# Counting edges tile by tile: each tile of 128 edges multiplied once, into PSUM banks of 50 destinations

## The reference

```python
HW = h @ W
row, col = (edge_index[0], edge_index[1])      # src, dst
s = HW @ a[:OUT_F, 0]
t = HW @ a[OUT_F:, 0]
e = leaky_relu(s[row] + t[col], 0.2)
m = segment_max(e, row)
ex = exp(e - m[row])
den = segment_sum(ex, row)
att = ex / den[row]
agg = segment_sum(att[:, None] * h[col], row)
basis = _b_splines(agg, grid)                  # 8 cubic splines on each feature
out = silu(agg) @ base_w.T + einsum('nip,oip->no', basis, spline_w)
x = layernorm(x + out)
```

## Time and profile before

| | us |
|---|---|
| median of 3 runs | 429.96 (428.74 to 430.42) |
| the profiled execution | 430.31 |
| its span, first to last instruction | 428.5 |

### The profile page before, as it was taken

One profiled execution on the slowest core, in us unless ns is written; L12 is line 12 of the kernel. 1 busy time (PEld: TensorE's weight loads), 2 busy tenths in 40 slices (PEclk: granted clock), 3 DMA queues, 4 the chain that ended last, 5 costly groups with the idle time before them and its releaser, 6 DMA issues.

```text
span 428.5 us, 5227 instructions
## 1 busy us (share of the span) xinstructions
PE 399.4 (93%) x1881; PEld 306.0 (71%) x1881; DVE 367.2 (86%) x457; ACT 274.0 (64%) x299; POOL 33.1 (8%) x162
## 2 busy tenths in 40 slices
PE   3999995299999999999999999999999999999994
PEld 0436563288888888878778888888777777777772
DVE  7968999997868867799988999989799969999645
ACT  7535675456456659788659586678646785779212
POOL 5100000100000000001100110101011010101000
PEclk9999999589999999999999999999999999999998
DMA  8980000600000000955454636363242346371303
GB/s 265 376 201 2 2 0 0 198 0 2 0 0 2 1 2 6 337 173 144 151 165 134 192 102 194 113 182 89 67 139 50 98 124 194 101 217 50 98 1 115
DMA packets 23452, 45.91 MB, mean 107 GB/s; under 512 B 1831, under 2 KB 2043, under 8 KB 23427
## 3 DMA queue, kind: packets, MB, share of 16 engines
q0 software_dynamic: 11088, 21.44, 18.6%
q1 hardware_dynamic: 12338, 24.14, 17.9%
HBM read 43.02 MB, written 2.56 MB: 106 GB/s over the span
## 4 chain that ended last, share of the span: by engine, by line
PE 54%; issue 29%; DVE 9%; POOL 3%; DMA 3%; ACT 0%; DVEq 0%; POOLq 0%
PE PS L1113 24%; PE PS L1069 17%; PE PS L1013 5%; POOL wh L374 3%; PE PS L1052 3%; DVE still L414 2%; DMA wh<-in_splT 2%; PE PS L989 2%; DVE oh L394 1%; DVE xl L502 1%; PE PS L968 1%; PE PS L1079 1%; DVE wl L593 1%; DMA ei<-in_edges 1%; DVE ex L629 0%
## 5 line engine op out<-in xcount | busy, mean ns | idle before, releaser
L1113 PE MATMUL PS<-wh,s 128*128 128x512 f32 (+1 forms) x720 | 225.2, 392 | 2.3 <-ACT s L884 1.1
L1113 PEld LDWEIGHTS PS<-wh,s 128*128 128x128 f32 (+1 forms) x720 | 133.4, 185 | 36.4 <-ACT s L884 3.5
L1113 PE MATMUL PS<-wl,s 128*128 128x512 f32 (+1 forms) x360 | 141.1, 392 | 0.0
L884 ACT ACTIVATE s<-v 128x1280 fp32r<-128x1280 f32 (+1 forms) x32 | 40.0, 1250 | 63.9 <-DVE v L701 58.9
L1113 PEld LDWEIGHTS PS<-wl,s 128*128 128x128 f32 (+1 forms) x360 | 66.8, 185 | 15.2
L1013 PE MATMUL PS<-oh,still 128*128 128x320 bf16 x304 | 45.4, 304 | 9.9 <-DVE still L414 7.9
L695 DVE SCALAR_TENSOR_TENSOR v<-v,v 128x1280 f32<-128x1280 f32 (+1 forms) x32 | 46.5, 1454 | 4.8 <-ACT v L870 4.8
L1013 PEld LDWEIGHTS PS<-oh,still 128*128 128x128 bf16 x304 | 28.8, 99 | 29.6 <-DVE still L414 9.6
L701 DVE SCALAR_TENSOR_TENSOR v<-v,v 128x1280 f32<-128x1280 f32 (+1 forms) x32 | 46.8, 1461 | 3.3
L711 DVE SCALAR_TENSOR_TENSOR s<-v,s 128x1280 fp32r<-128x1280 f32 (+1 forms) x32 | 46.5, 1454 | 0.6 <-ACT s L884 0.6
L697 DVE SCALAR_TENSOR_TENSOR v<-v,v 128x1280 f32<-128x1280 f32 (+1 forms) x32 | 46.5, 1454 | 0.0
(11 more groups left out here) (125 smaller groups left out, 374.4 us busy)
## 6 DMA issues: line engine op xcount, KB each, us to landing
wh<-in_splT POOLq DMA_DIRECT2D x32, 512.0 KB, 4.5
wring<-in_splT SPq DMA_DIRECT2D x21, 512.0 KB, 4.4
xt<-in_xT SPq DMA_DIRECT2D x1, 2500.0 KB, 11.6
xn<-in_x SPq DMA_DIRECT2D x1, 2304.0 KB
xh<-in_x POOLq DMA_DIRECT2D x1, 2304.0 KB, 13.3
out<-xr SPq DMA_DIRECT2D x9, 256.0 KB
wh<-in_baseT POOLq DMA_DIRECT2D x4, 512.0 KB, 5.3
wring<-in_baseT SPq DMA_DIRECT2D x3, 512.0 KB, 4.1
```

Of the source, the lines that this page charges most:

```text
L884: e.activation(parts(sh, u), bufs(u)[0], ACT.Relu).then_inc(s_shi, 1)
L1113: m = e.matmul(PS[0:rows(w), w % 8, :], sx[:, ic, tl * 128:tl * 128 + rows(w)], wx[:, ic, :], start=first and n == 0, stop=last and n == 2)
```

## The change

A window becomes 50 destinations instead of 32, with all ten high parts: 500 columns, one PSUM bank, 25 banks in all. The columns are ordered by destination first (`10 * dst + high part`), so that a tile of sorted edges falls in one constant stretch of columns, around `middle(t)` and `REACH` to each side (90 to 160). Each of 167 tiles is thus compared and multiplied once; where its stretch crosses the border of a bank, the matmul is cut in two (257 pieces, of 46,003 columns together). Since several tiles add to parts of a bank, a bank is set to zero first, by a matmul of zeros over 500 columns (`cleared`). `im` now runs from -160 to 159 and a key is `10 * dst + high - middle(t)`. `still` no longer depends on the window: one instruction for 8 tiles, 21 in all in place of 40, and the table `iq` that ACT built for it goes. DVE's keys go from six instructions to four, ACT writes the keys of `still`.

ACT reads a bank with a step of ten elements, since `C` and `Z` stay ordered by block and destination. The leftovers are now kept by tile: a tile whose least or greatest destination lies outside its stretch is counted in the loop. Their keys (10 instructions on all partitions) and their table (29 instructions on one partition) move to POOL, behind its DMAs of `xh`; DVE keeps three reductions and the scan, and waits for POOL at batches 10, 13 and 17. The work that PE does between windows is spread by batch instead. `x_low` stands behind batches 16 to 20, and five times behind the last.

```diff
-DW = 32
-ND = RP // DW
-MV = NT * DW
+DW = 50
+ND = N // DW
+CW = DW * NT
+MV = LW * NT
+MID, PER_TILE, PER_BATCH = 42, 75, 602
+REACH = [5 * (18, 22, 24, 26, 28, 30, 30, 32, 32, 32, 32)[min(b, NB - 1 - b)] for b in range(NB)]
+def middle(t):
+    return MID + PER_BATCH * (t // TB) + PER_TILE * (t % TB)
+def stretches(t):
+    lo, hi = max(middle(t) - REACH[t // TB], 0), min(middle(t) + REACH[t // TB], ND * CW)
+    return [(w, max(lo, CW * w), min(hi, CW * w + CW)) for w in range(lo // CW, (hi - 1) // CW + 1)]
...
+        ENDS_AT, LEAST_AT, SCAN_AT, SIZES_AT = 3, 10, 13, 17
+        X_LOW_AT = {16: 1, 17: 2, 18: 3, 19: 4, 20: 5}
+        TABLE = 29
...
+            e.wait_ge(s_edge, 16)
+            e.wait_ge(s_bits, 2)
+            e.wait_ge(s_setup, SETUP["reach"])
+            e.tensor_copy(left_place[:, :], ei[:, 1, :]).then_inc(s_left, 1)
+            e.tensor_copy(left_in[:, :], et[:, 0, :]).then_inc(s_left, 1)
+            e.wait_ge(s_left, 1)
+            e.tensor_scalar(left_col[:, :], left_place[:, :], float(NT), None, ALU.mult).then_inc(s_left, 1)
...
+            e.wait_ge(s_ends_r, 1)
+            e.tensor_scalar(wf[:, :, 0:NC], ends[:, :, :], 1 / LW, (1 - LW) / (2 * LW), ALU.mult, ALU.add).then_inc(s_tab, 1)
...
+            for k in range(2):
+                e.tensor_tensor(ways[:, k, :], ways[:, k, :], out_of[:, :], ALU.mult).then_inc(s_tab, 1)
+            e.wait_ge(s_least, 1)
...
-                if b >= RB:
-                    e.wait_ge(s_cw, last_window(b - RB) + 1)
+                if b >= RB:
+                    e.wait_ge(s_ct, done(b - RB))
...
+            for b in range(NB):
+                moving(b)
+                if b == 0:
+                    e.wait_ge(s_lk, 1)
+                one_hot_still(b)
...
+                if b == LEAST_AT:
+                    e.wait_ge(s_tab, 15)
+                    e.tensor_reduce(tu[:, 0:2], ways[:, :, :], AX.X, ALU.max).then_inc(s_least, 1)
+                if b == SCAN_AT:
+                    e.wait_ge(s_tab, 22)
...
+                if b == SIZES_AT:
+                    e.wait_ge(s_tab, TABLE)
...
+                ps = PS[:, w % 6, 0:CW].rearrange("p (b a) -> p a b", a=NT)
...
+            def cleared(w):
+                e.matmul(PS[:, w % 6, 0:CW], nought[:, 0:128], nought[:, :], start=True, stop=False)
...
-                for v in range(VIS[w]):
-                    m = e.matmul(PS[:, w % 6, 0:MV], still[:, w % RH, v, :], oh[:, (FIRST[w] + v) % (RB * TB), :],
-                                 start=(v == 0), stop=(v == VIS[w] - 1))
+                    for w, lo, hi in stretches(t):
+                        if w >= 6 and t == FIRST_TILE[w]:
+                            e.wait_ge(s_hole, w - 5)
+                            cleared(w)
+                        m = e.matmul(PS[:, w % 6, lo - CW * w:hi - CW * w], still[:, b % RB, t % TB, :],
+                                     oh[:, b % RB, t % TB, lo - o:hi - o], start=False, stop=(t == LAST_TILE[w]))
```

More of the change, by code:

```diff
@@ L45 @@
 SETUP = {n: k + 1 for k, n in enumerate(
-    ["im", "iq"] + [f"step{k}" for k in range(6)]
-    + ["bidx0", "bidx1", "wr", "zero", "id0", "ident", "xpad", "bigb", "wpad", "rest0", "rest1", "rest2", "rest3", "rest4",
-       "rest5", "visits"] + [f"bias{p}" for p in range(2 * NP + 1)])}
+    ["im", "mid", "nought", "id0", "ident", "xpad", "bigb", "wpad", "cpad"]
+    + [f"bias{p}" for p in range(2 * NP + 1)] + ["reachcol", "lplace"]
+    + [f"{n}{k}" for k in range(2) for n in ("sign", "mids", "ways", "window")] + ["turn", "rest", "zero", "begin", "reach"])}
 def build(nc, x, xT, edges, dstN, WT, a2, baseT, splT, out):
@@ L366, in _ @@
+            e.tensor_copy(r_size[:, 2:3], upto_rest[:, NC + 1:]).then_inc(s_tab, 1)
             for u in range(NU):
@@ L554, in _ @@
-            for w in range(4, NT):
-                x_low(w)
-            e.wait_ge(s_hole, ND)
-            with e.Fori(0, windows) as j:
-                _, (start, n0, n1, w) = nc.values_load_multi_w_load_instructions(
-                    r_rest[0:1, bass.ds(within(j, 0, NR), 1), :].rearrange("p a b -> p (a b)"), engines=[e.engine],
-                    min_val=-NR * NC, max_val=NR * NC, skip_runtime_bounds_check_because=CLAMPED)
-                w = within(w, 0, ND - 1)
-                d = bass.ds(w * DW, DW)
-                with e.Fori(within(n0, 0, NR * NC), within(n1, 1, NR * NC)) as n:
-                    tile = within(n + start, 0, NC)
+            e.tensor_scalar(et[:, 0, :], ei[:, 0, :], 7, None, ALU.arith_shift_right).then_inc(s_bits, 1)
@@ new lines, in _ @@
+            for k in range(len(X_LOW_AT), NT):
+                x_low(k)
+            e.wait_ge(s_left, 10)
+            with e.Fori(first, behind) as j:
+                tile = within(j, 0, NC)
+                _, (start, n0, n1) = nc.values_load_multi_w_load_instructions(
+                    r_rest[0:1, bass.ds(tile, 1), :].rearrange("p a b -> p (a b)"), engines=[e.engine],
+                    min_val=-LND * NC, max_val=LND * NC, skip_runtime_bounds_check_because=CLAMPED)
+                with e.Fori(within(n0, 0, LND * NC), within(n1, 1, LND * NC)) as n:
+                    w = within(n + start, 0, LND - 1)
+                    d = bass.ds(w * LW, LW)
+                    e.tensor_tensor(kk[:, :, :], left_key[:, bass.ds(tile, 1), :], lplace[:, bass.ds(w, 1), :],
+                                    ALU.subtract).then_inc(s_ovk, 1)
+                    e.tensor_tensor(one_still[:, :, :].rearrange("p k (m b) -> p k m b", b=2), places_of(1),
+                                    lk[:, bass.ds(tile, 1), :].unsqueeze(2).broadcast_to([128, 1, 64, 2]), ALU.is_equal
+                                    ).then_inc(s_ovs, 1)
+                    e.wait_ge(s_ovk, n + 1)
@@ L775, in _ @@
         def _(e):
[L776 to L781 removed]
+            e.wait_ge(s_bits, 2)
+            e.copy(lk[:, :, :], et[:, 1, :].unsqueeze(2).broadcast_to([128, NCP, 2])).then_inc(s_lk, 1)
             def st_rows(k):
```

460 lines of the change are left out of this document (209 added, 251 removed).

## The result

| | before | after |
|---|---|---|
| median of 6 runs each | 429.58 us (428.74 to 430.70) | 431.42 us (431.22 to 431.99) |
| ratio, 95% interval | | 1.0039 (1.0022 to 1.0057) |
| profiled execution, its span | 430.31, 428.5 | 431.29, 429.5 |
| start of `greatest(0)` | 76.24 | 78.48 |

The changed kernel is 0.4% slower, where 422.5 us was forecast: outside the range, and on the other side of no change. Counting ends 2.2 us later instead of 7.5 us earlier.

A forecast was written before the change was run, and what follows sets the result against it. DVE and PE together were taken to bound counting, with attention's tail constant. DVE's 53.7 us plus 4.6 + 7.0 + 3.4 gave attention's start at 68.7, 7.5 us earlier than 76.2: median 422.5 us, range 412 to 430.

The forecast's parts named there:

- From 16.35 us to DVE's wait some twelve get through: Counting, by turns: twelve POOL instructions finish before DVE's first table wait, delaying DVE by 4.6 us.
- turns: Counting: POOL reads and two-operand DVE instructions wait for each other; 53.7 + 4.6 + 7.0 + 3.4 = 68.7 us, chance 0.47.
- side by side: Counting: POOL and DVE read without conflict; 53.7 + 4.2 + 1.1 = 59.0 us to the start of attention.
- POOL's price: POOL's chain: 0.83 ns per element, 0.13 us fixed, two operands at twice the element price, 0.16 us per handover.
- The first rival: POOL and DVE reading without conflict: attention starts 17.2 us earlier, median 412.8 us; chance 0.32.
- The slower rival: POOL's instructions dearer and taking turns, all 39 on DVE's path: 434.1 us at 0.3 us more each; chance 0.11.
- I keep 4.9: Start of counting: DVE's first `oh` still starts at 4.9 us, two key instructions fewer but a handover to ACT more.
- DVE's own work: Counting on DVE with no wait at all: 48.8 us of work from 4.9 us, so `greatest(0)` starts at 53.7.
- ACT's step of ten elements: ACT's reads of PSUM banks: between nothing and some 15 us more; the lower end was taken.
- my floor: PE's count pieces: 0.071 to 0.109 us each at least, so 24.2 to 29.5 us instead of 21.0.
- The second rival: PE bounds counting, pieces never under 0.15 us: attention starts at 69, 422.8 us; chance 0.10 for PE or ACT.
- The tail: From the start of `greatest(0)` to the end of the span: taken as constant, 352.3 us.

The follow-up runs named there:

- Let in: Changed kernel plus three more short DVE waits, each for POOL's first instruction of a stretch: 427.41 us, ratio 0.9955 to the kernel before.
- the waits late: Changed kernel with all of DVE's waits for POOL's table moved behind the last batch: 423.38 us, ratio 0.9858 to the kernel before.

## Why the prediction was wrong

**The step that failed** is "From 16.35 us to DVE's wait some twelve get through". It took POOL and DVE as taking turns from the first instruction. The trace shows none of them through: L393 alone lasted until DVE stopped at 26.92. I had weighed two cases, side by side and turns, and the real one lay outside both: POOL stands still as long as DVE is ready, and DVE is ready until it waits for POOL. Then each wait is as long as all of POOL's work up to it. The form of the sum shows it: 53.5 own work, 1.15 late start, 24.1 of waits are 78.75 against 78.48 measured. I had 4.6 + 7.0 + 3.4 = 15.0 for what became 24.1, with DVE itself not slowed at all.

The Trainium skill, page "SBUF — State Buffer", section "Who interferes with whom", lets the second of the two wait for the whole of the first. The runs agree on who disturbs whom (two-operand reads of DVE, reads of POOL, not its writes). On how long they go beyond it: L393 waited for all of DVE's stream, and only behind a pause did the page's picture come.

**The term that was mis-sized** is POOL's price, by which it would have been slower than forecast even side by side. From 27.07 to 44.81 POOL ran free: 24 instructions in 17.7 us, where I had 13.8 for 25. I had scaled from an iota and a select, both of other kinds. An addition with one operand costs more than one with two (0.66 against 0.56 us for 176 elements), and so does the comparison of 336 (1.05 against 0.88), while I had taken the second operand as an extra; it is not so for every kind (the cast at L394 took 0.32 us, L416 with 336 elements 0.46). The handovers were cheaper than mine, some 0.08 us instead of 0.16. With a free start at 17.2 and this price POOL would reach `ways` at about 35, some 8 us behind DVE, not 4.2. The first rival, side by side, would then have been near 63, not 59.0. The last 14 instructions, free, sum to 5.3 us (L442 and L455 as in "Let in") where I had 3.4. Over the chain that is about 0.16 us more for each, an estimate; by my own rate, 0.19 us for each takes back the 7.5 us, turns with this price would have given about 75. So even with turns there was hardly a gain to forecast.

**The slower rival** had the right sign, and its range, 431 to 440, holds the 431.42 measured, but by luck. POOL's instructions were dearer, as it said; they did not take turns, and the time lost is in the standstill. Its chance of 0.11 was too small because I asked only how dear a read is, not whether it happens at all.

**Constants at the start.** "I keep 4.9" failed: 6.05. Before, POOL's constants at that moment were single elements and the shift took 0.25 us; now they fill 128 partitions, and it takes 1.60.

**What held.** `oh` 27.2 us and `still` 14.3 us, both to a tenth. DVE's own work 53.5 (53.7). ACT's step of ten elements costs next to nothing: 580 and 691 ns for 500 columns, where the count of elements gave 575 and 682. PE's pieces are cheaper than my floor. PE's timeline of after at the full clock (start, us, shape of the first of the group):

```profile
70.10 0.43 PE L1003 MATMUL PS<-nought 128*128 128x500 bf16 x1
70.37 0.93 PE L1017 MATMUL PS<-oh,still 128*128 128x56 bf16 x10
...
73.12 0.79 PE L1017 MATMUL PS<-oh,still 128*128 128x40 bf16 x11
```

Four clears and 40 pieces lie in 70.10 to 73.91 (in the first 0.2 us the clock is still at half): (3.81 - 4 x 0.215) / 40 = 0.074 us each. By the kernel's constants these 40 have 8 to 260 columns, 153 on average, and my price without any floor, the columns at 2.4 GHz and 7 ns, is 0.071 us. So no floor shows; the 0.109 us had come from float transposes. The second rival, PE as the bound, is out. The tail was 351.0 us, forecast 352.3, and 350.2 to 352.1 in the ten experiments.

**What stays open.** That the interference is between DVE's two-operand stream and POOL's reads rests on the memsets that got through, the reads that did not, and the moment at which each was let go; a stream of DVE instructions with one operand was not tried against POOL's reads. Why a pause in front of a two-operand instruction lets POOL in for good (until DVE's stream ends, 29 us on, with the waits late), while a reduction in between doesn't, is not settled. One idea, not tried: that DVE's next instruction is already on its way while the one ahead runs, and holds POOL off.

## What to carry to other kernels

Ahead of moving small work to POOL, ask who reads it and when: behind a DVE that runs two-operand instructions without a pause, POOL's reads may not move at all, and a DVE wait for their result then costs the chain's whole length, added up over its links and not hidden. The same 39 instructions cost DVE 8.4 us when it did them itself between its large ones, against 24.1 us of waiting. And when two cases for an unshown interaction are weighed, work out the worst one too, no progress whatever, when no trace row of "POOL reads beside a busy DVE" is at hand.

## What the runs showed of the hardware that was not expected

- A reading POOL instruction beside a ready stream of two-operand DVE instructions was kept out for up to 10.9 us, while DVE's durations stayed the same. One that was under way when the stream began ended at its own price (0.65 us). POOL's memsets in the same place took 0.27 us.
- After a pause of DVE of 0.2 to 0.6 us in front of a two-operand instruction, POOL's reads got through between DVE's: `oh` of 2560 elements went from 1.48 to as much as 1.85 us, `still` from 0.68 to as much as 1.38, a POOL read of 0.69 to 1.82.
- The other way round: back-to-back memsets of POOL over 128 partitions stretched a one-operand integer shift of DVE from 0.25 to 1.60 us; memsets of single elements, in before, did not. The Trainium skill, page "SBUF — State Buffer", section "Who interferes with whom", names DVE's faster modes as a case of its own; whether this shift runs in one no run here shows.
- Bf16 matmuls of 8 to 260 columns (153 on average), each with its own 128 columns of weights, took 0.074 us on average at 2.4 GHz, which is little more than their columns.
